# A graph network cell on one core: the scaling by the root and the beta of the layer normalisation, from VectorE to ScalarE and GpSimd

## The chip, the core and the metric

The kernel runs on one core of a Trainium2 chip. A core has five engines that run their own instruction streams and meet only at semaphores: TensorE (PE: matmuls into PSUM; its weight loads are shown as PEld), VectorE (DVE), ScalarE (ACT), GpSimd (POOL) and SyncE (SP, here the queue that issues nearly all DMAs). The metric is the time of one execution on the device in microseconds; less is better.

## What is computed

64 graphs of 128 nodes with 256 features each. Neighbours are averaged apart for each of four edge labels, a linear layer and relu follow, then a gated update, then a layer normalisation of each row of 256 values. The change touches the last line only.

```
weight = mask / (sum(mask) + EPS)                 # mask: adj == 1, 2, 3, 4
agg    = einsum('dbmn,bnh->bmdh', weight, hid)
out    = relu(linear(agg, Wd, bd))
r      = sigmoid(linear(out, Wri, bri) + linear(hid, Wrh, brh))
z      = sigmoid(linear(out, Wzi, bzi) + linear(hid, Wzh, bzh))
n      = tanh(linear(out, Wni, bni) + r * linear(hid, Wnh, bnh))
out    = (1 - z) * n + z * hid
return (out - mu) / sqrt(var + LN_EPS) * gamma + beta
```

## The kernel before

Graphs go in 32 pairs. The engines' streams are written out by hand, each as a function `step(i)`; `run_steps` calls it for 36 steps: steps 0 to 5 in line, then a hardware loop of 6 rounds of 4 steps (6 to 29), then steps 30 to 35 in line. A pair stays in the pipeline for five steps. In step `i` the kernel works on pair `i` (x times Wd, the y banks; counts; the label sums in `p_bank`), on pair `i - 1` (the transposes in `t_bank` and their split into `o_hi` and `o_lo`), on pair `q = i - 2` (the gate products in the banks `alpha`, `beta` and `gamma`), on `m = i - 3` (sigmoid, tanh, mixing) and on `j = i - 4` (the second half of the normalisation and the store). So step 31 is the last one with all of TensorE's work. Steps 32 and 33 have only gate products (and in 32 what is left of pair 31), and steps 34 and 35 have no work for TensorE.

The matmuls multiply fp32 numbers split in a high and a low part, three passes for each product. ScalarE makes the high parts (`y_hi` L448, `x_hi` L495, `o_hi` L511 and L547), VectorE (`y_lo` L592, `o_lo` L718) and GpSimd (`x_lo` L827, `o_lo` L864) the low ones.

Order on each engine is the order of the code, and a wait holds all that is behind it. The bank `mix` in PSUM holds both graphs of one pair, 2 x 256 columns: VectorE writes r times n's part into it (L690), later the mixed result (L726, from `z_part` and `n_sb`, both in SBUF), takes its statistics (L628, L633), and in the next step it subtracts the mean and multiplies by gamma in place (`norm_centre`, L649). GpSimd computes `from_n` (L840), `z_part` (L845), `o_lo` (L864), adds epsilon to the variance (L868) and raises it to -1/2 (`rstd`, L873). Then VectorE writes `normed` in SBUF, one instruction of 256 columns for each graph (L670), which reads `mix`, `rstd` and the beta rows, and SyncE stores the pair (L268). In a listing all these SBUF tiles that were cut out of one buffer carry the name `shared`: `z_part`, `n_sb`, `normed`, `c_sb`, `rz_sb` and the `u` tiles.

Around the place that matters ScalarE does, in a step: two scalings of `p_bank` (L456), the bias into `gamma` (L467), `y_hi` of the first half (L448), the copy of `alpha` into `beta` (L479), the sigmoid of both gates (L488, which waits for all four parts of `c_sb`; VectorE's L778 writes the last), `x_hi` (L495), `y_hi` of the second half (L448) and the tanh (L501).

Of the kernel before, what the change touches and what calls it, by code (L numbers as in the profile page):

```python
# [4 lines left out]
GRAPHS, N, H, D = 64, 128, 256, 4  # L5
# [3 lines left out]
LAG_GATES = 2  # L9
LAG_MIX = LAG_GATES + 1  # L10
LAG_NORM = LAG_MIX + 1
# [20 lines left out]
def gnn_kernel(nc, x, xT, adjT, wdT, wgT, bd, vectors, out):  # L32
    f32, f32r, bf16, i32 = mybir.dt.float32, mybir.dt.float32r, mybir.dt.bfloat16, mybir.dt.int32
    ALU, ACT = mybir.AluOpType, mybir.ActivationFunctionType

    ctx = ExitStack()
    with ctx:
# [6 lines left out]
        def sem(name):  # L44
            return ctx.enter_context(nc.semaphore(name))
# [145 lines left out]
        rstd_ready = sem("rstd_ready")  # L191
        scaled_ready = sem("scaled_ready")
        result_ready = sem("result_ready")

# [9 lines left out]
        def has_pair(k):  # L204
            return 0 <= k < PAIRS
# [18 lines left out]
        def _(sp):  # L224
# [21 lines left out]
            def step(i, up):  # L246
# [19 lines left out]
                if has_pair(j):  # L266
                    sp.wait_ge(result_ready, up(2 * j + 2, 2))
                    sp.dma_start(out[up(j)].rearrange("p (g f) -> p g f", g=2), normed[:, j % 2, :, :])\  # L268
                        .then_inc(stored[j % 2], 16)
# [145 lines left out]
        def _(act):  # L415
# [12 lines left out]
            def step(i, up):  # L428
                q, m = i - LAG_GATES, i - LAG_MIX

# [30 lines left out]
                if has_pair(q):  # L461
# [5 lines left out]
                    nc.scalar.activation(gamma[:, :], bias_step[:, :], ACT.Copy).then_inc(gamma_loaded, 1)  # L467
                y_high(0, 0)
                if i == 1:
                    weights_x(T2)  # L470
                    weights_o(B11)
# [101 lines left out]
        def _(dve):  # L573
# [12 lines left out]
            def step(i, up):  # L586
# [75 lines left out]
                if has_pair(i):  # L662
                    count_ratio(i)
                if has_pair(j):
                    dve.wait_ge(rstd_ready, up(j + 1))
                    if j >= 2:
                        dve.wait_ge(stored[j % 2], up(16 * (j // 2), 8))
                    for g in range(2):
                        dve.wait_ge(scaled_ready, up(2 * j + g + 1, 2))
                        nc.vector.scalar_tensor_tensor(normed[:, j % 2, g, :], mix[:, g * H:(g + 1) * H],  # L670
                                                       rstd[:, g:g + 1], vec_rows[:, beta_rows],
                                                       ALU.mult, ALU.add).then_inc(result_ready, 1)
                y_low(0, 0)
# [10 lines left out]
                if has_pair(m):  # L684
                    dve.wait_ge(rz_ready, up(m + 1))
                    if m >= 1:
                        dve.wait_ge(pre_ready, up(m))
                        dve.wait_ge(result_ready, up(2 * m, 2))

# [94 lines left out]
        def _(pool):  # L784
# [31 lines left out]
            def step(i, up):  # L816
                q, m = i - LAG_GATES, i - LAG_MIX

# [41 lines left out]
                if has_pair(i - 1):  # L860
                    pool.wait_ge(oshi_ready, up(i))
                    if i >= 4:
                        pool.wait_ge(p3_done, up(i - 2))
                    nc.gpsimd.tensor_tensor(*split_lo(o_lo[:, (i - 1) % 2, 3:7, :], o_sums[:, 1:5, :],  # L864
                                                      o_hi[:, (i - 1) % 2, 3:7, :])).then_inc(oslo_ready, 1)
                if has_pair(m):
                    pool.wait_ge(mv_ready, up(2 * m + 2, 2))
                    nc.gpsimd.tensor_tensor(var_eps[:, :], mean_var[:, :, 1], ln_eps[:, :], ALU.add)\  # L868
                        .then_inc(ve_ready, 1)
                    if m >= 1:  # L870
                        pool.wait_ge(result_ready, up(2 * m, 2))
                    pool.wait_ge(ve_ready, up(m + 1))
                    nc.gpsimd.tensor_tensor(rstd[:, :], var_eps[:, :], power[:, :], ALU.pow).then_inc(rstd_ready, 1)  # L873
# [44 lines left out]
```

## Time and profile before

| | before |
|---|---|
| median of 3 runs | 548.65 us (547.62 to 548.74) |
| profiled execution | 547.88 us |
| span of its trace | 546.1 us |
| TensorE busy | 512.1 us, 94% |
| VectorE busy | 436.0 us, 80% |
| ScalarE busy | 387.9 us, 71% |
| GpSimd busy | 301.4 us, 55% |
| mean granted clock of TensorE | 0.976 of full |

The span goes from the first to the last instruction; the profiled execution's own time has 1.8 us more around it. TensorE is above 90% busy in all slices of the page but the first two and the last three. In the trace a busy TensorE is not proof of a bound: matmuls overlap and their ends are modelled. Idle time is listed in brackets before the instruction that ended it, with the instruction that released it.

### The profile page before, as it was taken

How to read it: one execution, taken by the hardware profiler on the slowest of the kernel's cores; microseconds unless marked ns; L12 is line 12 of the kernel's file. 1: busy time of each engine (PE TensorE's matmuls, PEld its weight loads, DVE VectorE, ACT ScalarE, POOL GpSimd, SP SyncE). 2: the span in 40 equal slices, each digit the busy share in tenths (PEclk: the TensorE clock that was granted, in tenths of full speed). 3: DMA queues.
4: the chain of work that ended last, by engine and by line, in shares of the span. 5: the costliest groups of instructions: out<-in, count | busy, mean ns of one | idle time of the engine just before them, and what ended most of it. 6: DMA issues, size and time to landing. Idle time of an engine off the chain costs nothing.

```text
span 546.1 us, 10515 instructions
## 1 busy us (share of the span) xinstructions
PE 512.1 (94%) x3011; PEld 467.4 (86%) x3011; DVE 436.0 (80%) x1075; ACT 387.9 (71%) x725; POOL 301.4 (55%) x311
## 2 busy tenths in 40 slices
PE   4759999999999999999999999999999999999970
PEld 2548999999999999999999999999999999999860
DVE  5685688888888888888888888888888888888755
ACT  4366777777777777777777777777777777777651
POOL 5564555655565556556655566565555665653333
PEclk9688999999999999999999999999999999999996
DMA  8302022122111221222111211121112122110100
GB/s 283 111 30 68 1 68 69 49 69 68 68 50 39 67 67 48 67 67 67 51 36 67 67 48 67 67 67 56 35 63 67 49 66 67 38 38 29 40 31 38
DMA packets 19877, 33.42 MB, mean 61 GB/s; under 512 B 2224, under 2 KB 6576, under 8 KB 19856
## 3 DMA queue, kind: packets, MB, share of 16 engines
q1 hardware_dynamic: 19728, 32.78, 18.4%
q0 software_dynamic: 128, 0.39, 0.2%
q8 instruction: 9, 0.15, 0.1%
q14 instruction: 12, 0.10, 0.1%
HBM read 24.77 MB, written 8.39 MB: 61 GB/s over the span
## 4 chain that ended last, share of the span: by engine, by line
PE 88%; issue 3%; POOL 3%; DVE 3%; ACT 2%; DMA 1%; SPq 0%; POOLq 0%; DVEq 0%; ACTq 0%
PE y_bank L281 33%; PE alpha L281 23%; PE gamma L281 11%; PE p_bank L344 11%; PE beta L281 6%; PE t_bank L383 2%; DMA shared<-in_wdT 1%; PE t_bank L325 1%; DVE masks L645 1%; DVE y_lo L592 0%; POOL shared L840 0%; POOL shared L845 0%; POOL x_lo L827 0%; ACT y_hi L448 0%; ACT x_hi L495 0%
## 5 line engine op out<-in xcount | busy, mean ns | idle before, releaser
L827 POOL TENSOR_TENSOR x_lo<-x_f,x_hi 128x1024 fp32r<-128x1024 f32 x31 | 80.9, 2611 | 102.0 <-ACT x_hi L495 102.0
L448 ACT ACTIVATE y_hi<-y_bank 128x512 fp32r<-128x512 f32 x128 | 76.8, 600 | 63.7 <-PE y_bank L281 63.6
L281 PE MATMUL y_bank<-wd_hi,x_hi 128*128 128x512 f32 x256 | 106.1, 414 | 4.7 <-DVE wd_lo L580 4.7
L281 PE MATMUL y_bank<-wd_lo,x_hi 128*128 128x512 f32 x256 | 103.6, 405 | 0.0
L281 PE MATMUL y_bank<-wd_hi,x_lo 128*128 128x512 f32 x256 | 103.1, 403 | 0.0
L592 DVE TENSOR_TENSOR y_lo<-y_bank,y_hi 128x512 fp32r<-128x512 f32 x128 | 86.9, 679 | 13.9 <-ACT y_hi L448 13.8
L344 PE MATMUL p_bank<-y_hi,masks 128*128 128x256 f32 x256 | 68.0, 287 | 9.6 <-DVE y_lo L592 8.6
L864 POOL TENSOR_TENSOR o_lo<-o_sums,o_hi 128x512 fp32r<-128x512 f32 x32 | 41.4, 1295 | 52.8 <-ACT o_hi L547 52.8
L344 PE MATMUL p_bank<-y_lo,masks 128*128 128x256 f32 x256 | 67.6, 286 | 0.0
L456 ACT ACTIVATE p_bank<-p_bank,ratio 128x256 f32<-128x256 f32 x128 | 52.5, 456 | 11.0 <-PE p_bank L344 11.0
L281 PEld LDWEIGHTS y_bank<-wd_hi,x_hi 128*128 128x128 f32 x256 | 49.9, 195 | 12.0 <-issue 5.5
L281 PEld LDWEIGHTS y_bank<-wd_lo,x_hi 128*128 128x128 f32 x256 | 49.4, 193 | 11.6
L344 PEld LDWEIGHTS p_bank<-y_hi,masks 128*128 128x128 f32 x256 | 49.1, 192 | 11.6 <-issue 10.6
L281 PEld LDWEIGHTS y_bank<-wd_hi,x_lo 128*128 128x128 f32 x256 | 49.9, 195 | 6.0
L726 DVE TENSOR_TENSOR mix<-shared 128x512 f32<-128x512 f32 x32 | 22.4, 700 | 38.1 <-POOL shared L845 38.1
L840 POOL TENSOR_TENSOR shared<-x_rows,shared 128x512 f32<-128x512 f32 x32 | 41.5, 1298 | 19.6 <-ACT shared L501 19.6
L281 PE MATMUL alpha<-wx_hi,x_hi 128*128 128x384 f32 x128 | 46.7, 365 | 3.6 <-ACT shared L522 1.9
L344 PEld LDWEIGHTS p_bank<-y_lo,masks 128*128 128x128 f32 x256 | 49.3, 193 | 0.1
L281 PE MATMUL alpha<-wx_hi,x_lo 128*128 128x384 f32 x128 | 43.5, 340 | 0.0
L281 PE MATMUL alpha<-wo_hi,o_lo 128*128 128x384 f32 x128 | 43.4, 339 | 0.0
L281 PE MATMUL alpha<-wo_hi,o_hi 128*128 128x384 f32 x128 | 43.3, 339 | 0.0
L281 PE MATMUL alpha<-wx_lo,x_hi 128*128 128x384 f32 x128 | 43.3, 338 | 0.0
(116 smaller groups left out, 1357.2 us busy)
## 6 DMA issues: line engine op xcount, KB each, us to landing
x_f<-in_xT SPq DMA_DIRECT2D x32, 256.0 KB, 2.6
x_rows<-in_x SPq DMA_DIRECT2D x32, 256.0 KB, 3.0
out<-shared SPq DMA_DIRECT2D x32, 256.0 KB, 2.0
adj_in<-in_adjT SPq DMA_DIRECT2D x31, 128.0 KB, 2.4
shared<-in_wgT SPq DMA_DIRECT2D x2, 576.0 KB, 7.4
shared<-in_wdT SPq DMA_DIRECT2D x3, 256.0 KB, 6.4
vec_rows<-in_vectors SPq DMA_DIRECT2D x1, 512.0 KB, 8.4
x_rows<-in_vectors SPq DMA_DIRECT2D x1, 512.0 KB, 10.0
```

Of the source, the lines that this page charges most:

```text
L281: done = nc.tensor.matmul(dst, m, w, start=(first and t == 0), stop=(last and t == 2), skip_group_check=inside)
L325: last = nc.tensor.matmul(t_bank[:, g * D + d:g * D + d + 1], halves[:, d, :, 1], ones_bf[:, :], start=True, stop=True)
L344: last = nc.tensor.matmul(p_bank[:, b * H:(b + 1) * H], masks[:, k % 2, g, d, :], part[:, g, d * H:(d + 1) * H], start=first, stop=(part i ...
L383: last = nc.tensor.transpose(t_bank[:, (2 * g + c) * N:(2 * g + c + 1) * N], out_rows[:, g, c * N:(c + 1) * N], ident[:, :])
L448: nc.scalar.activation(y_hi[:, g, half(b)], y_bank[b][:, :], ACT.Copy)\
L456: nc.scalar.activation(p_bank[:, b * H:(b + 1) * H], p_bank[:, b * H:(b + 1) * H], ACT.Copy, scale=ratio[:, k % 2, g, b:b + 1]).then_inc(p ...
L592: nc.vector.tensor_tensor(*split_lo(y_lo[:, g, half(b)], y_bank[b][:, :], y_hi[:, g, half(b)]))\
L645: nc.vector.tensor_scalar(*label_masks(i + 1, d)).then_inc(masks_ready, 1)
L726: nc.vector.tensor_tensor(mix[:, :], z_part[:, :], n_sb[:, :], ALU.add).then_inc(mix_ready, 1)
L827: nc.gpsimd.tensor_tensor(*split_lo(x_lo[:, k % XRING, :, :], x_f[:, k % 2, :, :], x_hi[:, k % XRING, :, :])).then_inc(xlo_ready, 1)
L840: nc.gpsimd.tensor_tensor(from_n[:, :], x_rows[:, m % 2, :, :].rearrange("p g f -> p (g f)"), n_sb[:, :], ALU.subtract).then_inc(from_read ...
L864: nc.gpsimd.tensor_tensor(*split_lo(o_lo[:, (i - 1) % 2, 3:7, :], o_sums[:, 1:5, :], o_hi[:, (i - 1) % 2, 3:7, :])).then_inc(oslo_ready, 1)
```

## The change

VectorE's two instructions of L670 go. In their place ScalarE multiplies each half of `mix` by its column of `rstd` and writes `normed` (a Copy activation with a scale, 256 columns each; new semaphore `unit_ready`). It stands behind the first `y_hi` of the step and ahead of the copy into `beta`, and waits for `rstd`, for both centred halves and, from the third pair on, for the store that read this slot of `normed`. Then GpSimd adds the beta rows to both halves in one `tensor_tensor` of 512 columns, in place in `normed`, behind its `o_lo` and ahead of the variance. SyncE's store waits for that (`result_ready`, now one for a pair). The two users of `mix` and `rstd` that waited for the result now wait for `unit_ready`.

```diff
@@ SyncE
-                    sp.wait_ge(result_ready, up(2 * j + 2, 2))
+                    sp.wait_ge(result_ready, up(j + 1))
@@ ScalarE, behind y_high(0, 0)
+                if has_pair(j):
+                    act.wait_ge(rstd_ready, up(j + 1))
+                    act.wait_ge(scaled_ready, up(2 * j + 2, 2))
+                    if j >= 2:
+                        act.wait_ge(stored[j % 2], up(16 * (j // 2), 8))
+                    for g in range(2):
+                        nc.scalar.activation(normed[:, j % 2, g, :], mix[:, g * H:(g + 1) * H], ACT.Copy,
+                                             scale=rstd[:, g:g + 1]).then_inc(unit_ready, 1)
@@ VectorE, ahead of y_low(0, 0)
-                if has_pair(j):
-                    dve.wait_ge(rstd_ready, up(j + 1))
-                    if j >= 2:
-                        dve.wait_ge(stored[j % 2], up(16 * (j // 2), 8))
-                    for g in range(2):
-                        dve.wait_ge(scaled_ready, up(2 * j + g + 1, 2))
-                        nc.vector.scalar_tensor_tensor(normed[:, j % 2, g, :], mix[:, g * H:(g + 1) * H],
-                                                       rstd[:, g:g + 1], vec_rows[:, beta_rows],
-                                                       ALU.mult, ALU.add).then_inc(result_ready, 1)
@@ VectorE, ahead of r times n's part into mix
-                        dve.wait_ge(result_ready, up(2 * m, 2))
+                        dve.wait_ge(unit_ready, up(2 * m, 2))
@@ GpSimd, behind o_lo
+                if has_pair(j):
+                    pool.wait_ge(unit_ready, up(2 * j + 2, 2))
+                    nc.gpsimd.tensor_tensor(normed[:, j % 2, :, :], normed[:, j % 2, :, :],
+                                            vec_rows[:, beta_rows].unsqueeze(1).broadcast_to([128, 2, H]), ALU.add)\
+                        .then_inc(result_ready, 1)
                 if has_pair(m):
                     pool.wait_ge(mv_ready, up(2 * m + 2, 2))
                     nc.gpsimd.tensor_tensor(var_eps[:, :], mean_var[:, :, 1], ln_eps[:, :], ALU.add)\
                         .then_inc(ve_ready, 1)
                     if m >= 1:
-                        pool.wait_ge(result_ready, up(2 * m, 2))
+                        pool.wait_ge(unit_ready, up(2 * m, 2))
```

Added lines shift the numbers: L448 becomes L449, L479 becomes L488, L488 becomes L497, L649 becomes L658, L868 becomes L873 and L873 becomes L878.

ScalarE at the start of a step of the loop, before:

```order
L456 ACTIVATE p_bank<-p_bank,ratio 128x256 x2
L467 ACTIVATE gamma<-bias_step 128x512
L448 ACTIVATE y_hi<-y_bank 128x512
L479 ACTIVATE beta<-alpha 128x512
L488 ACTIVATE shared<-shared 128x1024
L495 ACTIVATE x_hi<-x_f 128x1024
```

and after:

```order
L457 ACTIVATE p_bank<-p_bank,ratio 128x256 x2
L468 ACTIVATE gamma<-bias_step 128x512
L449 ACTIVATE y_hi<-y_bank 128x512
L476 ACTIVATE shared<-mix,rstd 128x256 x2
L488 ACTIVATE beta<-alpha 128x512
L497 ACTIVATE shared<-shared 128x1024
L504 ACTIVATE x_hi<-x_f 128x1024
```

The two new scalings (L476) stand ahead of the copy into `beta`, the sigmoid and `x_hi`.

GpSimd in the last four steps, 32 to 35, before:

```order
L840 TENSOR_TENSOR shared<-x_rows,shared 128x512
L845 TENSOR_TENSOR shared<-shared 128x512
L864 TENSOR_TENSOR o_lo<-o_sums,o_hi 128x512
L868 TENSOR_TENSOR var_eps<-mean_var,ln_eps 128x2
L873 TENSOR_TENSOR rstd<-var_eps,power 128x2
L840 TENSOR_TENSOR shared<-x_rows,shared 128x512
L845 TENSOR_TENSOR shared<-shared 128x512
L868 TENSOR_TENSOR var_eps<-mean_var,ln_eps 128x2
L873 TENSOR_TENSOR rstd<-var_eps,power 128x2
```

(of steps 32 and 33; 34 is as 33, and 35 has nothing), and after, steps 33 to 35:

```order
L840 TENSOR_TENSOR shared<-x_rows,shared 128x512
L845 TENSOR_TENSOR shared<-shared 128x512
L868 TENSOR_TENSOR shared<-shared,vec_rows 128x512
L873 TENSOR_TENSOR var_eps<-mean_var,ln_eps 128x2
L878 TENSOR_TENSOR rstd<-var_eps,power 128x2
L840 TENSOR_TENSOR shared<-x_rows,shared 128x512
L845 TENSOR_TENSOR shared<-shared 128x512
L868 TENSOR_TENSOR shared<-shared,vec_rows 128x512
L873 TENSOR_TENSOR var_eps<-mean_var,ln_eps 128x2
L878 TENSOR_TENSOR rstd<-var_eps,power 128x2
L868 TENSOR_TENSOR shared<-shared,vec_rows 128x512
```

The new add (now L868) stands right behind `z_part` in steps 33 and 34, and alone in step 35.

VectorE in step 34, before:

```order
L649 SCALAR_TENSOR_TENSOR mix<-mix,mean_var,vec_rows 128x256 x2
L670 SCALAR_TENSOR_TENSOR shared<-mix,rstd,vec_rows 128x256 x2
L690 TENSOR_TENSOR mix<-shared 128x512
L697 TENSOR_TENSOR shared<-mix,shared 128x512
L726 TENSOR_TENSOR mix<-shared 128x512
```

and after:

```order
L658 SCALAR_TENSOR_TENSOR mix<-mix,mean_var,vec_rows 128x256 x2
L690 TENSOR_TENSOR mix<-shared 128x512
L697 TENSOR_TENSOR shared<-mix,shared 128x512
L726 TENSOR_TENSOR mix<-shared 128x512
```

VectorE goes from the centring straight to L690, which waits for ScalarE's sigmoid.

## Rows read from the trace of the kernel before

**Rows 1.** The page, part 1: busy time and share of the span.

```profile
PE 512.1 (94%) x3011; PEld 467.4 (86%) x3011; DVE 436.0 (80%) x1075; ACT 387.9 (71%) x725; POOL 301.4 (55%) x311
```

**Rows 2.** Busy time of each engine in two stretches (from:to, length, engines, clock, DMA).

```profile
246.45:262.02 15.57, 15.57 (x100) 14.41 (x97) 13.03 (x34) 11.79 (x23) 8.99 (x10) 1.00 0.18 59
...
533.21:546.10 12.89, 0.00 (x0) 0.00 (x0) 6.52 (x16) 1.69 (x2) 3.45 (x5) 0.66 0.11 41
```

**Rows 3.** The page, part 5: line engine op, tiles, count, busy, mean ns.

```profile
L670 DVE SCALAR_TENSOR_TENSOR shared<-mix,rstd,vec_rows 128x256 f32<-128x256 f32 x64 | 27.7, 471 | 0.2 <-POOL rstd L873 0.2
```

**Rows 4.** Timeline of ACT, step 15: start, us, instruction [idle before].

```profile
246.43 0.81 ACT L456 ACTIVATE p_bank<-p_bank,ratio 128x256 f32<-128x256 f32 x2 [0.28 <-PE p_bank L344]
247.16 0.60 ACT L467 ACTIVATE gamma<-bias_step 128x512 f32<-128x512 f32 x1
248.13 0.60 ACT L448 ACTIVATE y_hi<-y_bank 128x512 fp32r<-128x512 f32 x1 [0.37 <-PE y_bank L281]
249.18 0.58 ACT L479 ACTIVATE beta<-alpha 128x512 f32<-128x512 f32 x1 [0.45 <-PE alpha L281]
...
252.10 0.60 ACT L448 ACTIVATE y_hi<-y_bank 128x512 fp32r<-128x512 f32 x1 [0.42 <-PE y_bank L281]
```

**Rows 5.** Timeline of DVE near the end of that step.

```profile
260.13 0.67 DVE L592 TENSOR_TENSOR y_lo<-y_bank,y_hi 128x512 fp32r<-128x512 f32 x1
```

**Rows 6.** Timeline of PE near the end of that step.

```profile
261.34 0.28 PE L344 MATMUL p_bank<-y_hi,masks 128*128 128x256 f32 x1
```

**Rows 7.** Timeline of POOL at the end of that step and after.

```profile
261.51 0.20 POOL L868 TENSOR_TENSOR var_eps<-mean_var,ln_eps 128x2 f32<-128x2 f32 x1 [1.46 <-DVE mean_var L633]
...
263.06 0.74 POOL L805 TENSOR_TENSOR x_f<-x_f 128x256 f32<-128x256 f32 x1
```

**Rows 8.** Timeline of DVE, the ratio of the next step.

```profile
263.14 0.68 DVE L621 TENSOR_TENSOR ratio<-rcount,counts 128x4 f32<-128x4 f32 x1
```

**Rows 9.** Instructions of line 827 (GpSimd): shortest, median and longest.

```profile
L827 POOL TENSOR_TENSOR x_lo<-x_f,x_hi x31: 2355/2647/2659, 14.5 to 485.2; 128x1024 fp32r<-128x1024 f32 x31
```

**Rows 10.** Instructions of line 621 (VectorE), the same view.

```profile
L621 DVE TENSOR_TENSOR ratio<-rcount,counts x32: 158/626/689, 13.9 to 496.6; 128x4 f32<-128x4 f32 x32
```

**Rows 11.** Timeline of ACT in the last steps.

```profile
512.75 1.07 ACT L488 ACTIVATE shared<-shared 128x1024 f32<-128x1024 f32 x1
...
523.45 0.58 ACT L479 ACTIVATE beta<-alpha 128x512 f32<-128x512 f32 x1 [0.27 <-PE alpha L281]
...
533.54 1.06 ACT L488 ACTIVATE shared<-shared 128x1024 f32<-128x1024 f32 x1 [1.89 <-DVE shared L778]
```

**Rows 12.** Timeline of DVE in the last steps.

```profile
513.85 0.70 DVE L690 TENSOR_TENSOR mix<-shared 128x512 f32<-128x512 f32 x1
...
522.47 0.88 DVE L649 SCALAR_TENSOR_TENSOR mix<-mix,mean_var,vec_rows 128x256 f32<-128x256 f32 x2
...
529.89 0.70 DVE L726 TENSOR_TENSOR mix<-shared 128x512 f32<-128x512 f32 x1 [3.41 <-POOL shared L845]
...
533.21 0.87 DVE L649 SCALAR_TENSOR_TENSOR mix<-mix,mean_var,vec_rows 128x256 f32<-128x256 f32 x2
...
534.99 0.70 DVE L690 TENSOR_TENSOR mix<-shared 128x512 f32<-128x512 f32 x1
...
542.72 0.88 DVE L670 SCALAR_TENSOR_TENSOR shared<-mix,rstd,vec_rows 128x256 f32<-128x256 f32 x2 [0.23 <-POOL rstd L873]
```

**Rows 13.** Timeline of POOL in the last steps.

```profile
519.99 1.30 POOL L864 TENSOR_TENSOR o_lo<-o_sums,o_hi 128x512 fp32r<-128x512 f32 x1 [1.32 <-ACT o_hi L547]
521.25 0.20 POOL L868 TENSOR_TENSOR var_eps<-mean_var,ln_eps 128x2 f32<-128x2 f32 x1
521.59 0.69 POOL L873 TENSOR_TENSOR rstd<-var_eps,power 128x2 f32<-128x2 f32 x1
...
528.58 1.27 POOL L845 TENSOR_TENSOR shared<-shared 128x512 f32<-128x512 f32 x1
...
538.49 1.26 POOL L845 TENSOR_TENSOR shared<-shared 128x512 f32<-128x512 f32 x1
```

More of the change, by code:

```diff
@@ L192, in gnn_kernel @@
         scaled_ready = sem("scaled_ready")
+        unit_ready = sem("unit_ready")
         result_ready = sem("result_ready")
@@ L428, in step @@
             def step(i, up):
-                q, m = i - LAG_GATES, i - LAG_MIX
+                q, m, j = i - LAG_GATES, i - LAG_MIX, i - LAG_NORM
                 def weights_x(w):
@@ L816, in step @@
             def step(i, up):
-                q, m = i - LAG_GATES, i - LAG_MIX
+                q, m, j = i - LAG_GATES, i - LAG_MIX, i - LAG_NORM
                 def weights_o(w):
```

## The prediction

> **What bounds the kernel now.** I read the page first: TensorE is busy for 94% of the span [rows 1]. Then the busy time by step, to see whether that share is an average over unlike stages. It is: in step 15, which is like all from 4 to 31 and 15.57 us long, TensorE has no idle time at all, VectorE works 13.03 us, ScalarE 11.79 and GpSimd 8.99, while in the last 12.89 us TensorE does nothing [rows 2]. So the program has two parts. Up to the end of step 31 (511.0 us) TensorE sets the pace, and other engines matter only if they come late. In the 35 us behind it, steps 32 to 35, a chain passes from engine to engine, and each microsecond that is added to it is a microsecond of the result. The timelines of the engines then tell, for each place where the change puts or takes something, how long its engine had been idle there.
>
> **The steady steps.** *Removed from VectorE*: 64 instructions of 471 ns, 27.7 us in all [rows 3], 0.87 us for a pair. TensorE waits for nobody there, so this is worth 0. Nor does it move much: VectorE's next instruction is `y_lo`, which needs ScalarE's `y_hi` (248.73), so VectorE mostly waits there instead.
>
> *Added to ScalarE*: the nearest rows are the two scalings of `p_bank`, also 256 columns each with a scale for each row: started at 246.43, and the next instruction at 247.16, so a pair takes 0.73 us of the queue [rows 4]. The source is PSUM as there, the destination SBUF; I take 0.73 and bound it by 0.70 and 1.0 us. `y_hi` ends at 248.73, so the pair is through the queue by 249.46, where `alpha` into `beta` started at 249.18 after 0.45 us of idle time: 0.28 us late. Sigmoid and `x_hi` behind it are late by the same, and then comes `y_hi` of the second half, ahead of which ScalarE had 0.42 us idle [rows 4]: there the delay is gone. What the pair needs is ready: in the next step it would start at 248.73 + 15.57 = 264.30, while VectorE's ratio, which stands behind both centrings, started at 263.14 and GpSimd's L805, behind `rstd`, at 263.06 [rows 7, 8]. GpSimd's `x_lo` and what follows from it may be 0.28 us late; the tightest place for TensorE is `y_lo` of the last half, done at 260.13 + 0.67 = 260.80 [rows 5], which TensorE needed at 261.34 [rows 6]. 0.54 us of slack against 0.28: worth 0.
>
> *Added to GpSimd*: one operation of 512 columns, as L864 and L845, 1.27 to 1.30 us [rows 13]. Behind `o_lo` the engine was idle for 1.46 us until the variance came [rows 7]. It fits, and `rstd` is as early as before. The store leaves some 12 us later in the step, but SyncE's next load only comes in the following step, and the slot of `normed` is needed two steps on: worth 0. Cover for both: ScalarE's 0.45 + 0.42 us and GpSimd's 1.46 us; without them a step costs 0.73 or 1.29 us. Sum for 28 steps: 0.
>
> **Step 32.** No `y_hi` here. The pair stands ahead of `alpha` into `beta`, and right behind that the sigmoid started at 512.75 without idle time and VectorE's L690 at 513.85, as soon as it ended [rows 11, 12]. So all that follows on ScalarE, and the chain, is late by the pair: **+0.73**. GpSimd's `o_lo` ends at 521.29 + 0.73 = 522.02 and now the add comes ahead of the variance, where there was no idle time: `rstd` ended 0.99 us behind `o_lo` (521.59 + 0.69 = 522.28) [rows 13] and now ends 1.25 more behind it, at 524.26.
>
> **Step 33.** ScalarE's pair must wait for both centred halves (522.47 + 0.88 + 0.73 = 524.08) and for `rstd` (524.26) [rows 12, 13]. It starts at 524.28, the copy into `beta` 0.73 later at 525.01 instead of 523.45 [rows 11]: the chain is **1.56** late. It ran over the sigmoid, tanh, `from_n` and `z_part` to L726, and nothing between them had room.
>
> **GpSimd's add against L726.** `z_part` ended at 528.58 + 1.27 = 529.85 and VectorE's L726, which waits for it and reads two SBUF tiles, started at 529.89, 0.04 later [rows 12, 13]. Behind `z_part` GpSimd now has the add, and nothing that it waits for is missing. Do the two engines disturb each other? The ratio (L621, four columns, two SBUF sources) takes 158 ns at best and 626 in the median [rows 10]; in the row it started at 263.14, 0.08 after GpSimd's L805, and ended at 263.82, 0.02 after that ended (263.80) [rows 7, 8]. And `x_lo` on GpSimd takes 2355 ns at best, 2647 in the median [rows 9]. So a VectorE operation with two SBUF sources and a GpSimd one exclude each other; the later one ends its own length less 0.14 us after the earlier. Who is first? GpSimd starts an operation that has nothing to wait for 0.04 us before the record of the last one ends: 521.25 against 519.99 + 1.30 = 521.29 [rows 13]. That is 0.08 us ahead of L726. I take GpSimd first: the add runs to 1.25 us behind `z_part`, L726 ends 0.70 - 0.14 = 0.56 later, at 1.81, where it ended at 0.04 + 0.70 = 0.74: **+1.07**, chain 2.63 late. Ends: 0 if VectorE is first, 1.25 if nothing of it overlaps.
>
> The Trainium skill, on the page "SBUF — State Buffer", section "SBUF: two separate sides", has this as a rule: VectorE and GpSimd share a pair of ports under an exclusive lock, a VectorE operation with two SBUF inputs needs it against a GpSimd one that reads SBUF, and whichever starts first holds it for its whole instruction. The rows of L621 and L805 agree. By the rule alone it is the order of starts that decides 1.07 us, twice.
>
> **Step 34.** VectorE's centred halves end at 533.21 + 0.87 + 2.63 = 536.71. Before, the sigmoid (533.54) did not depend on them; now it stands behind the pair, which does. Pair at 536.74, sigmoid at 537.49, its end at 538.55, L690 at 538.57 against 534.99 [rows 11, 12]: **3.58** late. VectorE's freed 0.87 us helps nothing, since L690 waits for the sigmoid. Then `z_part` and the add against L726 again: **+1.07**, 4.65 late.
>
> **Step 35.** `rstd` released L670 at 542.72 [rows 12], so now it comes at 547.33; the pair (0.81 as the two rows of `p_bank`) ends at 548.18, the add at 549.5, and the store follows. Before, the two of VectorE ended at 542.72 + 0.88 = 543.60 [rows 12]. In all **+5.9 us**: 547.88 + 5.9 = 553.8 for the profiled execution. The median of the runs shown is 0.8 above that execution, the lowest 0.3 below; I say 554.0.
>
> **The rivals.**
>
> *A, VectorE first at L726.* The margin of 0.08 us is small, and no row shows such a close meeting. If VectorE is first, the add is pushed behind by some 0.7 us, into GpSimd's idle time ahead of the variance: in step 34 `z_part` ended at 539.75 and the variance, some 1 us ahead of the 542.72 of L670, began 1.9 us later [rows 12, 13], so an add of 1.3 us, 0.6 late, costs nothing. Then the chain is 1.56 late in step 33; step 34: halves 535.64, sigmoid 536.42, L690 537.50, 2.51 late; the end 547.37 against 543.60, +3.8: 551.6, or 552.4 from the median. If it is first in one of the steps only, +4.8: 552.7.
>
> *B, the steady steps lose.* The pair is longer than its 0.87 us of cover and the delay reaches `y_lo` of the last half and eats 0.54 us. Against it: rows of this kind are 0.73. A loss of 0.2 us in 28 steps is 5.6 us, so 559.4.
>
> *C, TensorE's records hide waits for VectorE (not slower).* Their ends are modelled, so 15.57 us without a gap could hold waits. VectorE is the busiest of the others and loses 0.87 us in a step. From 4.8/28 = 0.17 us a step on, the end's loss is outweighed to within 0.2%. With half of the 0.87, 12.2 us: 541.6. Against it: the step has the same length to 0.01 us, 15.56 or 15.57, wherever it is measured, and VectorE is idle for over 2 us of it.
>
> *D, only the last add counts.* If ScalarE's pair found room in steps 32 to 34 that the rows don't show, +1.3 for the add in step 35: 549.2.
>
> **How the numbers follow.** Forecast 0.50; A in both steps 0.27, in one 0.10; B 0.07; C 0.03; D 0.03. The range takes in the forecast and A (0.87) with their bounds: 551.0 to 556.0. A measurement of this kernel can tell 0.2%, 1.1 us, from no change. Slower by more than that: forecast, A, B less a little, 0.93. Same: D and a part of C, 0.05. Faster: 0.02.
>
> **What the profile after would show.** Steady steps of 15.56 us with a full TensorE, up to 511 us; VectorE 27 us less busy, ScalarE some 29 more, GpSimd 41 more. The sigmoid of step 34 right behind ScalarE's pair. L726 in steps 33 and 34 at 1.8 us instead of 0.70 in its record, or, by A, 0.70 and the add at 1.9. A last add of 1.3 us ahead of the last store. What would prove me wrong: longer steps (B), shorter ones (C), or a last stretch, from 511 us to the end, that grew by less than 3 us.

## The result and the profile after

| | before | after |
|---|---|---|
| median of 4 executions | 548.65 us | 555.5 us |
| ratio, 95% interval | 1 | 1.0126 (1.0106 to 1.0146) |
| profiled execution | 547.88 us | 555.35 us |
| span of its trace | 546.1 us | 553.6 us |
| VectorE, ScalarE, GpSimd busy | 436.0, 387.9, 301.4 us | 415.4, 408.4, 336.4 us |

The kernel became slower by about 7 us; the prediction was 554.0 (551.0 to 556.0), slower. One execution each of the changed kernel (2845.89 us) and of short_end_filler below (1767.09 us) was in a slow state; the ratios leave it out, and without it the two medians are 555.35 and 544.25 us instead of 555.5 and 544.86. Busy times, after, from the page:

```profile
PE 514.7 (93%) x3011; PEld 469.4 (85%) x3011; DVE 415.4 (75%) x1011; ACT 408.4 (74%) x789; POOL 336.4 (61%) x343
```

Work moved as the change says. VectorE lost 20.6 us of busy time, ScalarE gained 20.5, GpSimd 35.0. The prediction had 27, 29 and 41. It added up the records of the instructions, and busy time counts overlapping records once; besides, the two longest L726 (below) cost VectorE 2.1 us, and `x_lo` takes GpSimd 4.8 us less in all (76.1 instead of 80.9). The two new groups, by line:

```profile
L868 POOL TENSOR_TENSOR shared<-shared,vec_rows 128x512 f32<-128x512 f32 x32 | 41.5, 1297 | 0.9 <-ACT shared L476 0.9
...
L476 ACT ACTIVATE shared<-mix,rstd 128x256 f32<-128x256 f32 x64 | 26.7, 472 | 10.6 <-POOL rstd L878 7.1 <-DVE mix L658 3.6
```

**The steady steps.** The answer to [rows 2] is one row, the same window of the trace after:

```profile
246.45:262.02 15.57, 15.57 (x96) 14.41 (x95) 12.35 (x32) 12.44 (x25) 10.07 (x10) 1.00 0.17 59
```

TensorE is again busy for all of the 15.57 us. ScalarE's timeline of step 15 stands 0.64 us later on the trace's clock than in [rows 4]:

```profile
248.77 0.60 ACT L449 ACTIVATE y_hi<-y_bank 128x512 fp32r<-128x512 f32 x1 [0.38 <-PE y_bank L282]
249.26 0.83 ACT L476 ACTIVATE shared<-mix,rstd 128x256 f32<-128x256 f32 x2
249.97 0.61 ACT L488 ACTIVATE beta<-alpha 128x512 f32<-128x512 f32 x1
...
251.44 1.06 ACT L504 ACTIVATE x_hi<-x_f 128x1024 fp32r<-128x1024 f32 x1
252.72 0.60 ACT L449 ACTIVATE y_hi<-y_bank 128x512 fp32r<-128x512 f32 x1 [0.23 <-PE y_bank L282]
```

The pair follows the first `y_hi`, takes 0.71 us of the queue, and ScalarE still had 0.23 us idle ahead of the second `y_hi`. GpSimd has the add where it was idle, and waits 0.19 us for the variance instead of 1.46 [rows 7]:

```profile
260.63 1.30 POOL L868 TENSOR_TENSOR shared<-shared,vec_rows 128x512 f32<-128x512 f32 x1
262.12 0.20 POOL L873 TENSOR_TENSOR var_eps<-mean_var,ln_eps 128x2 f32<-128x2 f32 x1 [0.19 <-DVE mean_var L642]
```

The tight place of [rows 5, 6], VectorE's last `y_lo` and TensorE's first product that needs it:

```profile
260.75 0.67 DVE L601 TENSOR_TENSOR y_lo<-y_bank,y_hi 128x512 fp32r<-128x512 f32 x1
```

```profile
261.95 0.28 PE L345 MATMUL p_bank<-y_hi,masks 128*128 128x256 f32 x1
```

`y_lo` is done at 261.42, TensorE takes it up at 261.95: 0.53 us, where it was 0.54 before. Nothing was eaten, although `x_hi` was late: it starts 2.67 us behind the first `y_hi` (251.44 - 248.77), and started 2.49 behind it before (250.62 - 248.13). GpSimd gave these 0.18 us back. Its `x_lo` starts while VectorE's L690 still runs, which reads two SBUF tiles: the two records overlap by 0.39 us before (L690 to 252.14, `x_lo` from 251.75) and by 0.20 after (252.78 and 252.58), and `x_lo` takes 2.66 us before and 2.45 after.

**Behind 511 us.** The chain is slower from the first step on. Two rows of the trace before from which the next paragraphs count, the start of step 32 and VectorE's L778 of step 33:

```profile
511.02 0.81 ACT L456 ACTIVATE p_bank<-p_bank,ratio 128x256 f32<-128x256 f32 x2 [0.28 <-PE p_bank L344]
```

```profile
532.60 0.69 DVE L778 TENSOR_TENSOR shared<-gamma,shared 128x512 f32<-128x512 f32 x1 [0.46 <-PE gamma L281]
```

Timelines after, ScalarE, VectorE and GpSimd, the lines that answer to [rows 11 to 13]:

```profile
511.58 0.81 ACT L457 ACTIVATE p_bank<-p_bank,ratio 128x256 f32<-128x256 f32 x2 [0.28 <-PE p_bank L345]
...
514.06 1.06 ACT L497 ACTIVATE shared<-shared 128x1024 f32<-128x1024 f32 x1
...
525.58 0.60 ACT L488 ACTIVATE beta<-alpha 128x512 f32<-128x512 f32 x1
...
538.30 0.84 ACT L476 ACTIVATE shared<-mix,rstd 128x256 f32<-128x256 f32 x2 [3.58 <-DVE mix L658]
539.03 1.05 ACT L497 ACTIVATE shared<-shared 128x1024 f32<-128x1024 f32 x1
...
548.88 0.84 ACT L476 ACTIVATE shared<-mix,rstd 128x256 f32<-128x256 f32 x2 [6.69 <-POOL rstd L878]
```

```profile
532.00 1.76 DVE L726 TENSOR_TENSOR mix<-shared 128x512 f32<-128x512 f32 x1 [3.39 <-POOL shared L845]
...
536.73 0.69 DVE L778 TENSOR_TENSOR shared<-gamma,shared 128x512 f32<-128x512 f32 x1 [1.43 <-PE gamma L282]
...
540.11 0.70 DVE L690 TENSOR_TENSOR mix<-shared 128x512 f32<-128x512 f32 x1 [1.90 <-ACT shared L497]
...
544.91 1.74 DVE L726 TENSOR_TENSOR mix<-shared 128x512 f32<-128x512 f32 x1 [3.37 <-POOL shared L845]
```

```profile
530.70 1.26 POOL L845 TENSOR_TENSOR shared<-shared 128x512 f32<-128x512 f32 x1
531.92 1.28 POOL L868 TENSOR_TENSOR shared<-shared,vec_rows 128x512 f32<-128x512 f32 x1
...
543.62 1.26 POOL L845 TENSOR_TENSOR shared<-shared 128x512 f32<-128x512 f32 x1
544.83 1.26 POOL L868 TENSOR_TENSOR shared<-shared,vec_rows 128x512 f32<-128x512 f32 x1
...
549.80 1.26 POOL L868 TENSOR_TENSOR shared<-shared,vec_rows 128x512 f32<-128x512 f32 x1 [0.95 <-ACT shared L476]
```

The first row of ScalarE is the start of step 32, the two scalings of `p_bank`. They began at 511.02 before, so this trace is 0.56 us late there; the experiments show that to be chance. Counted from there, the sigmoid of step 32 is 0.75 us late, the copy into `beta` of step 33 1.57 us, L778 of step 33 3.57, L690 of step 34 4.56, and the last add ends (551.06) 6.90 us later than VectorE's last instruction did (543.60). L726 stands in two rows with 1.76 and 1.74 us; the median of its 32 instances is 0.70.

### The profile page after: what moved, and what is told of

The parts are those of the page before. It is cut to its first block, busy times and chain, and to the rows that moved or that the text cites. A ratio compares the mean times of both kernels' runs of the same rounds, so it can differ in the third digit from the quotient of the medians.

```text
span 553.6 us, 10517 instructions
## 1 busy us (share of the span) xinstructions
PE 514.7 (93%) x3011; PEld 469.4 (85%) x3011; DVE 415.4 (75%) x1011; ACT 408.4 (74%) x789; POOL 336.4 (61%) x343
## 4 chain that ended last, share of the span: by engine, by line
PE 87%; issue 4%; POOL 3%; DVE 3%; ACT 2%; DMA 1%; POOLq 0%; SPq 0%; ACTq 0%; DVEq 0%
PE y_bank L282 32%; PE alpha L282 23%; PE gamma L282 11%; PE p_bank L345 11%; PE beta L282 6%; PE t_bank L384 2%; DMA shared<-in_wdT 1%; PE t_bank L326 1%; DVE masks L654 1%; DVE y_lo L601 0%; POOL shared L840 0%; POOL shared L845 0%; POOL x_lo L827 0%; POOL rstd L878 0%; ACT y_hi L449 0%
## 5 line engine op out<-in xcount | busy, mean ns | idle before, releaser
L827 POOL TENSOR_TENSOR x_lo<-x_f,x_hi 128x1024 fp32r<-128x1024 f32 x31 | 76.1, 2454 | 107.9 <-ACT x_hi L504 107.9
L449 ACT ACTIVATE y_hi<-y_bank 128x512 fp32r<-128x512 f32 x128 | 76.7, 599 | 58.9 <-PE y_bank L282 58.9
L726 DVE TENSOR_TENSOR mix<-shared 128x512 f32<-128x512 f32 x32 | 24.5, 766 | 38.1 <-POOL shared L845 38.1
L282 PE MATMUL alpha<-wo_lo,o_hi 128*128 128x384 f32 x128 | 43.5, 340 | 0.0
```

The lines of the kernel that those rows point to most:

```text
L282: done = nc.tensor.matmul(dst, m, w, start=(first and t == 0), stop=(last and t == 2), skip_group_check=inside)
L449: nc.scalar.activation(y_hi[:, g, half(b)], y_bank[b][:, :], ACT.Copy)\
L726: nc.vector.tensor_tensor(mix[:, :], z_part[:, :], n_sb[:, :], ALU.add).then_inc(mix_ready, 1)
L827: nc.gpsimd.tensor_tensor(*split_lo(x_lo[:, k % XRING, :, :], x_f[:, k % 2, :, :], x_hi[:, k % XRING, :, :])).then_inc(xlo_ready, 1)
```

## The experiments

The steady steps and the last ones are compared apart. The **tail** is the time from the start of the scalings of `p_bank` in step 32 to the end of the last instruction ahead of the last store: 543.60 - 511.02 = 32.58 us before, 551.06 - 511.58 = 39.48 after.

| kernel | median us | ratio, 95% interval | tail us | against before |
|---|---|---|---|---|
| before | 547.85 to 548.04, beside each group of runs | 1 | 32.58 | 0 |
| after_again | 555.13 | 1.0133 (1.0110 to 1.0156) | 39.47 | +6.89 |
| steady_only | 548.22 | 1.0003 (0.9989 to 1.0017) | 33.63 | +1.05 |
| tail_only | 554.19 | 1.0123 (1.0090 to 1.0156) | 39.78 | +7.20 |
| add_late | 554.28 | 1.0100 (1.0066 to 1.0133) | 38.03 | +5.45 |
| filler | 554.02 | 1.0123 (1.0096 to 1.0149) | 38.53 | +5.95 |
| pair_late34 | 552.97 | 1.0106 (1.0073 to 1.0139) | 38.02 | +5.44 |
| pair_twice | 567.47 | 1.0359 (1.0331 to 1.0386) | 39.95 | +7.37 |
| add_late_filler | 551.41 | 1.0077 (1.0058 to 1.0095) | 36.55 | +3.97 |
| before_filler | 547.64 | 1.0002 (0.9990 to 1.0013) | 32.59 | +0.01 |
| short_end | 545.87 | 0.9967 (0.9948 to 0.9986) | 31.57 | -1.01 |
| short_end_filler | 544.86 | 0.9945 (0.9927 to 0.9962) | 30.10 | -2.48 |

Single executions of the kernel before lie between 546.15 and 549.56 us, and a median of four can be off by 1 us; where 1 or 2 us are at stake the tail of the profiled execution is the sharper number, but it is one execution. The tail of the changed kernel was taken twice (39.48 and 39.47); that of the kernel before once, and once more in before_filler (32.58 and 32.59).

### after_again: the changed kernel once more

> The changed kernel once more, on the chip of the next three, as their yardstick. 555.5 us, 1.0126 times the kernel before. If the 0.6 us by which its trace was behind at step 32 belong to the steady steps, they come again in the trace; if they are chance of the first 60 us, the steps are again 15.56 us and the start of step 32 moves by some tenths either way.

1.0133, tail 39.47 us: the loss behind step 32 repeats to 0.01 us. Step 32 began at 511.94. Over all profiled kernels it began anywhere from 509.64 (add_late_filler) to 511.95 (add_late), 510.26 in pair_late34 and 510.65 in tail_only. These have the same or nearly the same steady steps, so the 0.56 us of the first comparison are chance of the start, not a cost of the change.

### steady_only and tail_only: one half of the change each

```diff
+        def new_way(k):
+            return k < 28            # steady_only; in tail_only: k >= 28
-                if has_pair(j):
+                if has_pair(j) and new_way(j):           # ScalarE's pair, GpSimd's add
...
+                if has_pair(j) and not new_way(j):       # VectorE's two instructions
```

> Pairs 0 to 27 (steps 4 to 31) go the new way, over ScalarE and GpSimd, pairs 28 to 31 (steps 32 to 35) the old one, on VectorE. Theory (the steady steps lose and win nothing, everything is lost behind 511 us): as the kernel before, 548.6 us, ratio 1.000 within 0.002. Rival (the new way costs some hundredths of a us in each steady step, which the 0.6 us at step 32 would be): 549.2 us or more, ratio 1.001 to 1.002.

> The reverse: pairs 0 to 27 the old way, pairs 28 to 31 the new one. Theory: as the changed kernel, 555.5 us, and step 34's sigmoid 4.6 us later behind the start of step 32 than in the kernel before. Rival (part of the loss comes from the steady steps): 554.9 us or less.

steady_only has 28 of the 32 pairs on the new path and measures 1.0003, 0.9989 to 1.0017. tail_only has four on it and measures as the changed kernel. So the steady steps are worth nothing within 0.2%, and the loss sits in the last four steps. The median of tail_only alone, 554.19 us, would also fit its rival (554.9 or less); it is the ratio of steady_only that rules the rival out. The sigmoid of step 34 came 5.23 us later than before in tail_only, not 4.6; in the changed kernel it is 4.93. steady_only's tail is 1.05 us longer with instructions as before; the reason appears below (TensorE's clock in step 32, which fell in tail_only too).

### add_late: does the add meet L726?

```diff
-                if has_pair(j):
+                if has_pair(j) and i < 32:
                     pool.wait_ge(unit_ready, up(2 * j + 2, 2))
                     nc.gpsimd.tensor_tensor(...)         # the add
...
                     nc.gpsimd.tensor_tensor(rstd[:, :], var_eps[:, :], power[:, :], ALU.pow).then_inc(rstd_ready, 1)
+                if has_pair(j) and i >= 32:
+                    pool.wait_ge(unit_ready, up(2 * j + 2, 2))
+                    nc.gpsimd.tensor_tensor(...)         # the add
```

> The changed kernel with GpSimd's add of steps 32 to 35 moved behind the root, so that in steps 33 and 34 it no longer meets VectorE's L726. Theory (the two exclude each other): L726 is back from 1.75 to 0.70 us in its record, each step is 1.07 us shorter, the root of step 32 is 1.25 us earlier (0.17 us on the chain), 555.5 - 2.3 = 553.2 us. Rival (L726 is long for another reason, say its place behind z_part): L726 stays at 1.75 us, 555.3 us. The product of T4 and that of gamma in step 33, in which TensorE ran at the lower clock in the changed kernel, should stay slow: the gaps ahead of them are older than the add.

VectorE's L726 of steps 33 and 34, and GpSimd's adds (here L881) of steps 34 and 35, pairs 30 and 31, which the view puts into one row:

```profile
533.76 0.70 DVE L726 TENSOR_TENSOR mix<-shared 128x512 f32<-128x512 f32 x1 [3.39 <-POOL shared L845]
...
544.64 0.70 DVE L726 TENSOR_TENSOR mix<-shared 128x512 f32<-128x512 f32 x1 [3.37 <-POOL shared L845]
```

```profile
547.50 2.48 POOL L881 TENSOR_TENSOR shared<-shared,vec_rows 128x512 f32<-128x512 f32 x2
```

L726 is back at 0.70 us in both steps, with the same place behind `z_part`, so it was the add beside it that held it up, and the rival falls. The total is a miss: 554.28 us and not 553.2, tail 1.44 us shorter and not 2.3. TensorE's timeline shows where the rest is:

```profile
522.89 0.52 PE L282 MATMUL gamma<-wx_hi,x_hi 128*128 128x384 f32 x1
```

0.52 us in the record, at a spacing of 0.32 us, where at the upper clock it is 0.34 and 0.175: T4's and gamma's last product of step 32 ran mostly at the lower clock, and VectorE's L778 behind them waited 2.26 us for TensorE, and 0.73 in the changed kernel. So 1.5 us were lost there, while the 0.95 us of step 33 that are described next were not: the expectation that the products of step 33 stay slow missed too. That is 0.6 of the missing 0.9 us; 0.24 more are the edit's own cost (see add_late_filler). The five executions of add_late also differ: one took 550.45 us at a mean granted clock of 0.981, the other four 552.16 to 554.80 us at 0.964 to 0.971. That fits a clock that falls in some executions and not in others; only one of them has a trace.

### filler: TensorE's clock in the last steps

In the changed kernel the last two products of step 33 were slow (a product is six matmuls of 384 columns). TensorE, after_again (the trace of after has the same), the first matmul of T3's product and the first two of T4's, with the idle time ahead in brackets:

```profile
530.16 0.44 PE L282 MATMUL alpha<-wx_hi,x_hi 128*128 128x384 f32 x1 [1.20 <-ACT shared L531]
...
532.16 0.69 PE L282 MATMUL alpha<-wx_hi,x_hi 128*128 128x384 f32 x1 [0.69 <-ACT shared L544]
532.65 0.52 PE L282 MATMUL alpha<-wx_hi,x_lo 128*128 128x384 f32 x1
```

The stretch from 530 to 535 us, in after_again and in before (the number behind the engines is the mean granted clock):

```profile
530.00:535.00 5.00, 3.84 (x13) 3.02 (x14) 2.64 (x4) 1.70 (x4) 3.48 (x3) 0.70 0.11 42
```

```profile
530.00:535.00 5.00, 2.34 (x12) 1.70 (x10) 4.38 (x12) 1.66 (x2) 0.89 (x2) 1.00 0.00 0
```

In after_again the granted clock was 0.70 there and 0.50 from 535 to 540 us, and the spacing of the matmuls went from 0.175 to 0.32 us. In the 5 us ahead TensorE had been busy for 3.58 us, with gaps of 0.38 and 1.20 us. The kernel before had been busy for 3.29 of the same 5 us and kept the clock at 1.00 up to 535 us.

```diff
+            def filler(count):
+                pe.wait_ge(ylo_ready[0], 2 * PAIRS)
+                for _ in range(count):
+                    nc.tensor.matmul(y_bank[0][:, :], x_hi[:, 3, 0, :], wd_hi[:, 0, half(0)], start=True, stop=True)
...
+                    if i >= 32:                              # ahead of T3
+                        filler(6 if i == 32 else 4)
...
+                    if i >= 32:                              # ahead of T4
+                        filler(2)
...
+                    if i == 33:                              # ahead of gamma's last product
+                        filler(4)
```

> The changed kernel with matmuls that compute nothing needed, put into TensorE's idle time in step 32 (6 ahead of T3, 2 ahead of T4) and 33 (4, 2, and 4 ahead of gamma's last product), into a y bank that is free by then. Theory (in step 33 the chain lost 0.94 us because TensorE had dropped to its lower clock): the clock stays at its upper level to the last product, no matmul of 384 columns is over 0.44 us in its record, VectorE's L778 of step 33 comes 0.9 us earlier, 554.2 us. Rival (the clock falls whatever TensorE does, or the fillers come in its way): 555.1 us or more.

```profile
530.65 0.63 PE L296 MATMUL y_bank<-wd_hi,x_hi 128*128 128x512 f32 x2
531.50 0.44 PE L282 MATMUL alpha<-wx_hi,x_hi 128*128 128x384 f32 x1 [0.22 <-ACT shared L555]
...
534.12 0.44 PE L282 MATMUL gamma<-wx_hi,x_hi 128*128 128x384 f32 x1 [0.37 <-DVE shared L751]
```

```profile
535.47 0.69 DVE L789 TENSOR_TENSOR shared<-gamma,shared 128x512 f32<-128x512 f32 x1 [0.46 <-PE gamma L282]
```

The matmuls of 384 columns have 0.44 us and less in their records, the clock stayed up. VectorE's L778 (here L789) of step 33 came 12.63 us behind that of step 32 (522.84); in the changed kernel it was 13.58 (536.73 - 523.15). That is 0.95 us, and the tail is 0.95 us shorter. It is then 5.95 us longer than before, the 5.9 of the prediction. In total times the difference (554.02 against 555.13) is within their scatter, so the claim rests on the traces: one with these matmuls, two of the changed kernel without, and the other pairs of traces counted up at the end.

### pair_late34: the order on ScalarE in step 34

```diff
-                if has_pair(j):
+                if has_pair(j) and i != 34:
                     act.wait_ge(rstd_ready, up(j + 1))                    # the pair
...
                     nc.scalar.activation(rz_sb[:, :, :, :], c_sb[:, :, :, 128:GATE], ACT.Sigmoid).then_inc(rz_ready, 1)
+                if i == 34:
+                    act.wait_ge(rstd_ready, up(j + 1))                    # the pair
```

> The changed kernel with ScalarE's pair of step 34 behind the sigmoid instead of ahead of it. Theory (the term of step 34 is that the sigmoid of 1.06 us stands behind a pair that waits for both centred halves): the sigmoid runs beside the centring, L690 follows the pair, and the chain is 0.9 us shorter: 554.2 us. Rival (L690 waits for mix to be read in either order): 555.1 us.

```profile
535.41 1.06 ACT L497 ACTIVATE shared<-shared 128x1024 f32<-128x1024 f32 x1 [2.95 <-DVE shared L786]
536.37 0.82 ACT L504 ACTIVATE shared<-mix,rstd 128x256 f32<-128x256 f32 x2
```

```profile
537.33 0.70 DVE L698 TENSOR_TENSOR mix<-shared 128x512 f32<-128x512 f32 x1 [1.37 <-ACT shared L504]
```

The sigmoid starts without the centred halves, the pair follows it, and L690 (here L698) comes 2.86 us behind L778 (534.47); it was 3.38 in the changed kernel (540.11 - 536.73) and 2.39 in the kernel before. So the order is worth 0.52 us, not 0.9: L690 must still wait until the pair has read `mix`. The clock did not fall in this execution. 6.90 - 0.95 - 0.52 = 5.43, measured 5.44 us.

### pair_twice: how much room the steady steps have

```diff
+                    if i < 32:
+                        for g in range(2):
+                            nc.scalar.activation(normed[...], mix[...], ACT.Copy, scale=rstd[...]).then_inc(again_ready, 1)
+                        act.wait_ge(again_ready, up(2 * j + 2, 2))
                     for g in range(2):
                         nc.scalar.activation(normed[...], mix[...], ACT.Copy, scale=rstd[...]).then_inc(unit_ready, 1)
```

> The changed kernel with ScalarE's pair done twice in the steps before 32 (the same values into the same place, GpSimd waits for the second). Theory (ScalarE's idle time covers the pair): a second pair of 0.73 us makes y_hi of the second half about 0.5 us late, which is caught up before the next y_hi, since TensorE needs what hangs on it 1 us later: the steady steps stay at 15.56 us, 555.1 us. Rival (the cover ends with the first pair): 0.2 to 0.5 us a step, 561 to 569 us.

567.47 us, 12.3 us more than after_again, about 0.45 us in each of 28 steps, as the rival had it: a step is 16.03 us long (`y_hi` of the first half at 253.33 and, in the next step, at 269.36). The theory was wrong, and the trace shows the route that it had left out. ScalarE, GpSimd, VectorE and TensorE of one step:

```profile
253.33 0.60 ACT L450 ACTIVATE y_hi<-y_bank 128x512 fp32r<-128x512 f32 x1 [0.36 <-PE y_bank L283]
253.82 0.83 ACT L478 ACTIVATE shared<-mix,rstd 128x256 f32<-128x256 f32 x2
254.69 0.84 ACT L482 ACTIVATE shared<-mix,rstd 128x256 f32<-128x256 f32 x2
```

```profile
258.01 2.41 POOL L833 TENSOR_TENSOR x_lo<-x_f,x_hi 128x1024 fp32r<-128x1024 f32 x1 [3.70 <-ACT x_hi L510]
```

```profile
263.08 0.70 DVE L732 TENSOR_TENSOR mix<-shared 128x512 f32<-128x512 f32 x1 [1.54 <-POOL shared L851]
...
266.13 0.67 DVE L607 TENSOR_TENSOR y_lo<-y_bank,y_hi 128x512 fp32r<-128x512 f32 x1
```

```profile
266.33 0.34 PE L283 MATMUL gamma<-wo_lo,o_hi 128*128 128x384 f32 x1
266.91 0.36 PE L346 MATMUL p_bank<-y_hi,masks 128*128 128x256 f32 x1 [0.24 <-issue]
```

Against the first `y_hi`, `x_lo` starts 0.87 us later than in the changed kernel (258.01 - 253.33 = 4.68 against 3.81), VectorE's mixing behind `z_part` (L732 here) 0.83 later, and the last `y_lo`, which stands behind it in VectorE's queue, 0.82 later. TensorE had 0.53 us there. The row of 266.91 shows what is left over: TensorE was ready at 266.67, idle 0.24 us, and started 0.11 us behind the end of `y_lo` (266.80); in the code this matmul waits for `y_lo` of both halves. The profile names no releaser for it. The second `y_hi` is 0.54 us late (4.49 us behind the first instead of 3.95), and the `y_hi` after it no longer (8.36 against 8.37): that much of the theory held. So ScalarE's delay reaches TensorE over `x_hi`, GpSimd and VectorE's queue, not over `y_hi`. Of the 0.87 us of delay a step lost 0.46, so the cover is 0.4 us of delay, not ScalarE's idle time of 0.87.

### add_late_filler: both causes away at once

> The changed kernel without two of the causes at once: GpSimd's add of the last steps behind the root, and matmuls that compute nothing needed in TensorE's gaps of steps 32 and 33. Theory (the loss behind 511 us is the sum of ScalarE's pairs and the last add, 3.8 us, VectorE held up twice, 2.1 us, and TensorE's lower clock, 0.9 us): 548.0 + 3.8 = 551.8 us, ratio 1.007, no matmul at the lower clock up to the last product. Rival (the parts overlap or there is one more): 553 us or more.

Its edits are those of add_late and filler, with no matmuls ahead of gamma's last product. 551.41 us, 1.0077, tail +3.97 us, with no product at the lower clock up to the end. That is the 3.8 us that the prediction worked out for its rival A (VectorE not held up), plus 0.2. The end of the trace shows where these come from, ScalarE's last pair and GpSimd's last two adds:

```profile
543.77 0.84 ACT L485 ACTIVATE shared<-mix,rstd 128x256 f32<-128x256 f32 x2 [5.65 <-POOL rstd L887]
```

```profile
543.71 2.48 POOL L890 TENSOR_TENSOR shared<-shared,vec_rows 128x512 f32<-128x512 f32 x2
```

Moved behind the root, the add of step 34 now stands directly ahead of the last one. The pair ends at 544.61, and the last add, 1.26 us long, ends at 546.19, so it starts 0.32 us behind the pair; in the changed kernel it was 0.08. This 0.24 us is a cost of the edit. On the other side step 33's pair starts 13.13 us behind the start of step 32 instead of 13.27, since the add of step 32 is out of the way too. Without both, the pairs and the last add come to about 3.86 us. VectorE held up twice is 1.06 + 1.04 us by the records of L726, the clock 0.95: together 6.9, the measured difference. So the parts add up.

### before_filler: the kernel before with the clock held up

> The kernel before with such matmuls (3 and 2 in step 32, 3 and 2 in step 33). Its own profiled execution had TensorE at the upper clock in both steps, but its runs spread from 546.2 to 549.6 us. Theory (in some executions the clock falls in step 32 or 33, at up to 1.5 us each): the upper end of the spread goes, median 547.2 us, ratio 0.9975 to 0.999. Rival (the spread comes from the first 60 us): same spread, ratio 1.000.

1.0002, tail 32.59 against 32.58, spread 546.75 to 549.27 us against 546.52 to 549.35. The theory falls: the clock in steps 32 and 33 is not what spreads the runs of the kernel before, and filling TensorE's gaps is worth nothing where it does not fall. The rival fits: the two profiled executions, 547.88 and 546.75 us, are 1.13 us apart, and their starts of step 32 (511.02 and 509.87) are 1.15 apart. What moves that start was not looked into.

### short_end and short_end_filler: a shorter end for the kernel before

```diff
+                if i in (33, 34):                        # ScalarE, behind the bias copy: r's sigmoid apart
+                    nc.scalar.activation(rz_sb[:, :, 0, :], c_sb[:, :, 0, 128:GATE], ACT.Sigmoid).then_inc(r_ready, 1)
...
+                if i in (33, 34):                        # VectorE, ahead of L726 (its waits left out here)
+                    nc.vector.tensor_tensor(from_n[...], x_rows[...], n_sb[...], ALU.subtract).then_inc(from_ready, 1)
+                    nc.vector.tensor_tensor(z_part[...], rz_sb[:, :, 1, :], from_n[...], ALU.mult).then_inc(zpart_ready, 1)
...
-                if has_pair(m):                          # GpSimd's from_n and z_part
+                if has_pair(m) and i not in (33, 34):
```

> The kernel before (not the changed one) with its end shortened: in steps 33 and 34 VectorE itself computes from_n and z_part (0.70 us each instead of 1.27 on GpSimd), and the sigmoid of r runs as soon as its two parts are there, apart from that of z. Theory (behind 511 us the chain alone counts): step 33 0.9 us shorter by the sigmoid and 0.4 by z_part, since the gate product behind it limits the rest, step 34 1.2 us shorter by z_part: 548.2 - 2.5 = 545.7 us, ratio 0.9955. Rival (the end hangs on TensorE's products): 547.5 us or more.

> short_end with the matmuls (3 and 2 in step 32, 0 and 2 in step 33). In its profiled execution the products of T4 and gamma in step 32 ran at the lower clock, and VectorE's L778 of step 32 came 1.5 us later behind the bias copy than in the kernel before. Theory: that goes, 545.9 - 1.5 = 544.4 us, ratio 0.9935. Rival (that execution was an exception): 545.7 us, ratio 0.996.

Step 34 on VectorE, `from_n`, `z_part` and the mixing in a row:

```profile
537.57 0.69 DVE L740 TENSOR_TENSOR shared<-x_rows,shared 128x512 f32<-128x512 f32 x1 [0.70 <-ACT shared L510]
538.29 0.69 DVE L744 TENSOR_TENSOR shared<-shared 128x512 f32<-128x512 f32 x1
539.02 0.70 DVE L750 TENSOR_TENSOR mix<-shared 128x512 f32<-128x512 f32 x1
```

short_end: 0.9967, short_end_filler: 0.9945 (0.9927 to 0.9962), the fastest of all, faster than both kernels. Its tail is 2.48 us shorter, the 2.5 that was worked out, and in the steps that it was worked out for: L778 of step 33 comes 1.25 us earlier behind the start of step 32 (20.33 against 21.58), the rest is step 34. Without the fillers 1.5 of them went to the lower clock in step 32, and the tail is 1.01 shorter. In total times the two are not told apart (their intervals overlap).

## Why the prediction was right, and what it missed

*The steady steps cost nothing.* Right, shown by steady_only. The working held too: at the second `y_hi` the delay was gone (3.95 us behind the first, 3.97 before). For the other route, over `x_hi` to the last `y_lo`, it allowed 0.28 us. Measured, 0.18 us reached `x_hi`, because the pair starts 0.11 us ahead of the end of `y_hi`'s record (249.26 against 249.37) and not at it, and nothing reached the last `y_lo`, because `x_lo` became 0.2 us shorter, which the prediction did not see. pair_twice shows that this is the route by which ScalarE's delay gets to TensorE, with 0.4 us of room. The forecast named the place and its 0.54 us; it was the later expectation of pair_twice that forgot it. Only the cover that the forecast names, 0.87 us of ScalarE's idle time, was too much: pair_twice has 0.4. B falls with steady_only.

*Step 32, +0.73, and step 33, 1.56.* Measured 0.75 and 1.57. The pair took 0.72 to 0.73 us of ScalarE's queue, as the scalings of `p_bank` do.

*The add against L726, +1.07 in steps 33 and 34.* Measured: L726 took 1.76 and 1.74 instead of 0.70. The question who is first was decided as the rows said: the add starts at 531.92 and 544.83, 0.04 us ahead of the end of the record of `z_part`, L726 at 532.00 and 544.91, 0.08 behind it. So it was in all twelve meetings in the six traces that have them: L726 started 0.07 or 0.08 us behind the add and took 1.74 to 1.77 us. add_late shows that it is the add that does it. Rival A, at 0.27, did not come about, but had the right price: it is what add_late_filler measures.

*Step 34, 3.58 late.* Measured 4.56. The order on ScalarE is as forecast; pair_late34 shows that 0.52 us of it go with another order. The missing 0.95 us came earlier, in step 33; in filler, where the clock stayed up, L690 of step 34 is 3.61 us late.

*The term that was not there.* The prediction let TensorE's products in steps 32 and 33 run as fast as before, without a reason given; this is the term that it lacks. In the changed kernel TensorE fell to its lower clock for the last two products of step 33; 4.65 became 5.60, 5.9 became 6.9. filler shows it: with the gaps filled 5.95 remain. Where the clock falls is not steady from kernel to kernel: in step 33 in after and after_again, in step 32 in steady_only, tail_only, add_late, pair_twice and short_end (there 1 to 1.5 us), nowhere in before and pair_late34. So it fell in seven of nine traces without the added matmuls and in none of the four with them. pair_late34 has the changed kernel's gaps in both steps and kept the clock, so the longer gaps alone don't decide it. What does is open, and so is how often the changed kernel loses these 0.95 us: both of its traces do.

*C and D.* With VectorE relieved in 28 steps, steady_only is not faster (0.9989 to 1.0017, at most 0.02 us a step), so no wait for VectorE of that size is hidden in TensorE's steady steps. The last add is not all (add_late_filler). Both fall.

*The total.* 553.8 for the profiled execution, measured 555.35. Of the 1.5 us missing, 0.95 are the clock, 0.56 the start of step 32, which is chance. That the range up to 556.0 held the result is partly luck: no part of it stood for the clock.

## What to carry to other kernels

Where one engine is full for nine tenths of the time, as here, taking work from the second busiest can gain nothing, and the stretch without that engine decides: follow the moved work through the last steps, instruction by instruction. Ask of an operation that is put on GpSimd what VectorE starts at the same moment: where the two followed the same event here, the one that stood in its queue without a wait was ahead by 0.08 us, every time. And cover is not the idle time of the engine itself (0.87 us here), but the room on the tightest of all routes from it to the engine that is full (0.4 us here).

## What the runs showed of the hardware

- A VectorE operation with two SBUF sources beside a GpSimd one that started 0.08 us earlier took 1.76 us instead of 0.70 and ended 0.56 us behind it, its own length less 0.14. It is the rule of the Trainium skill, page "SBUF — State Buffer", section "SBUF: two separate sides" (the one that starts first holds the shared ports for its whole instruction); this trace agrees.
- TensorE fell from 2.4 to 1.2 GHz (granted clock 1.00 to 0.50) in the last steps of six kernels, behind gaps of 0.3 to 1.7 us, and the spacing of matmuls of 384 columns went from 0.175 to 0.32 us. That cost 0.95 to 1.5 us on the chain. In the four traces with 7 to 18 matmuls into an unused bank it stayed up, and in before_filler, where it had been up anyway, they cost nothing that can be measured (tail 32.59 us against 32.58).
